# A first depthwise convolution on TensorE: two taps a matmul from stacked copies of the padded image

## The reference

```
xin = jnp.einsum('bchw,oc->bohw', x, in_proj_w)
xc = jax.nn.silu(_dwconv(xin, conv2d_w, conv2d_b))
x1 = _dwconv(xc, dw_w, dw_b)
```

## Time and profile before

| what | value |
|---|---|
| three executions | 2455.08, 2449.93, 2454.44 us |
| median | 2454.44 us |
| the profiled execution | 2455.15 us |
| its span, first to last instruction | 2453.3 us |
| mean granted TensorE clock | 0.941 of full speed |
| TensorE busy | 2144.5 us (87%) |
| VectorE busy | 1864.1 us (76%) |
| first depthwise convolution, first pair | about 484 to 592 us |

### The profile page before, as it was taken

One profiled execution on the slowest core, in us unless ns is written; L12 is line 12 of the kernel. 1 busy time (PEld: TensorE's weight loads), 2 busy tenths in 40 slices (PEclk: granted clock), 3 DMA queues, 4 the chain that ended last, 5 costly groups with the idle time before them and its releaser, 6 DMA issues. The chain is left out here.

```text
span 2453.3 us, 28912 instructions
## 1 busy us (share of the span) xinstructions
PE 2144.5 (87%) x7243; PEld 1122.6 (46%) x7243; DVE 1864.1 (76%) x3251; ACT 1434.4 (58%) x2268; POOL 1412.1 (58%) x1287
## 2 busy tenths in 40 slices
PE   2998869898998999997988987698979799999798
PEld 2397635443453444433335964353435334444243
DVE  6556767589986999995755668565999589999754
ACT  1843444286884777773346446335868567777632
POOL 2232008488977999982322400393989399999532
PEclk9989989999998999998997998799999899999899
DMA  5000192500001222225810005634000012212344
GB/s 188 1 1 1 48 339 82 176 39 0 1 1 23 43 44 57 44 52 161 232 41 0 1 0 195 215 106 166 1 1 1 11 22 44 61 39 56 91 119 114
DMA packets 199338, 172.76 MB, mean 70 GB/s; under 512 B 72535, under 2 KB 175327, under 8 KB 195831
## 3 DMA queue, kind: packets, MB, share of 16 engines
q1 hardware_dynamic: 199159, 170.78, 24.3%
HBM read 81.69 MB, written 72.29 MB: 63 GB/s over the span
## 5 line engine op out<-in xcount | busy, mean ns | idle before, releaser
L942 POOL TENSOR_TENSOR BIG<-BIG 128x512 f32<-128x512 f32 x320 | 407.1, 1272 | 91.9 <-DVE BIG L850 73.5
L850 DVE TENSOR_TENSOR BIG<-PSUM,BIG 128x512 f32<-128x512 f32 x576 | 390.8, 681 | 61.0 <-PE PSUM L1061 35.5
L1133 DVE SCALAR_TENSOR_TENSOR PSUM<-BIG,VECS,PSUM 128x1024 f32<-128x1024 f32 x224 | 288.2, 1286 | 37.0 <-PE PSUM L2112 31.8
L776 POOL TENSOR_TENSOR BIG<-TOEP,BIG 128x384 f32<-128x384 f32 x84 | 98.0, 1194 | 320.2 <-DVEq L1558 320.2
L1069 PE MATMUL PSUM<-BIG,CSTS 128*128 128x512 f32 x512 | 264.9, 598 | 0.0
L2112 PE MATMUL PSUM<-BIG,WDW 128*128 128x512 f32 x512 | 233.0, 599 | 13.8 <-ACT BIG L2012 13.8
L1061 PE MATMUL PSUM<-BIG,SELB 120*128 120x512 bf16 x576 | 210.6, 384 | 16.9 <-issue 10.1
L2291 PE MATMUL PSUM<-BIG 128*128 128x381 f32 (+1 forms) x576 | 189.4, 492 | 12.9 <-DVE BIG L783 12.9
L1061 PEld LDWEIGHTS PSUM<-BIG,SELB 120*128 120x128 bf16 x576 | 55.1, 96 | 262.0 <-DVE BIG L850 163.3
L2112 PEld LDWEIGHTS PSUM<-BIG,WDW 128*128 128x128 f32 x512 | 97.1, 192 | 141.0 <-issue 115.0
L1785 POOL TENSOR_TENSOR BIG<-BIG 128x1024 f32<-128x1024 f32 x64 | 151.0, 2360 | 10.3 <-POOL BIG L1788 10.3
(11 more groups left out here) (365 smaller groups left out, 5170.9 us busy)
## 6 DMA issues: line engine op xcount, KB each, us to landing
spill<-X SPq DMA_DIRECT2D x18, 1024.0 KB, 5.9
back_spill<-BIG SPq DMA_DIRECT2D x32, 576.0 KB, 3.4
X<-x SPq DMA_DIRECT2D x32, 512.0 KB, 7.9
rows_spill<-X SPq DMA_DIRECT2D x64, 256.0 KB, 4.0
out<-BIG SPq DMA_DIRECT2D x64, 256.0 KB, 3.6
BIG<-rows_spill SPq DMA_DIRECT2D x28, 512.0 KB, 5.2
X<-back_spill SPq DMA_DIRECT2D x14, 896.0 KB, 11.7
BIG<-fc SPq DMA_DIRECT2D x8, 1024.0 KB, 10.3
```

Source lines behind the costliest of these rows:

```text
L776: eng.tensor_tensor(to.rearrange("p (x c r) -> p x c r", x=3, r=WROW), TOEP[:, y].unsqueeze(1).unsqueeze(1).broadcast_to([P, 3, WCH, WROW] ...
L850: dve.tensor_tensor(img(product_buffer(b, q)), img(PSUM[:, (k + q) % 2, :]), pch(c, XBASE, dy, dx), ALU.mult).then_inc(df_p, 1)
L942: pool.tensor_tensor(a, a, x, ALU.add).then_inc(df_add, 1)
L1133: return dve.scalar_tensor_tensor(out=rows8(to), in0=strip(c, base, dy, dx), scalar=vc(weights, j), in1=rows8(acc), op0=ALU.mult, op1=ALU.add)
```

## The change

Taps 0 and 1 of every strip now go to TensorE together with taps 3 and 4. For each strip, four DMAs on SP's queue copy PAD rows into a buffer `STK[c % 2]`, each 64 partitions by 8 rows of 130 elements: for image q, partitions 0 to 63 get the rows shifted up by one and partitions 64 to 127 get the rows themselves. A matmul over 128 partitions with the weights `WSTK` (128 x 64: the diagonal of tap j above, that of tap j + 3 below) then sums two taps of one image into 64 partitions of PSUM. The two images go to the two halves of TensorE's columns, in turn. TensorE waits for the DMAs (`moved`) in place of `in_cp`. The DMAs of strip c wait for `in_cp` of that strip and for `d1_mm` of strip c - 2. Four of the nine reloads of X are issued at once as before, the other five stand one each behind the copies of strips 0 to 4.

ScalarE keeps two side taps, 2 and 5, GpSimd one addition. VectorE has taps 6, 7, 8 and the side sum in every strip, and waits for `in_cp` of the strip below itself. The buffers are placed anew in REG, and the counts of the semaphores change with them.

```diff
-SIDE_TAPS = 3
-DW1_VECTOR, DW2_VECTOR = (4, 5), (5, 6)
+DW1_STACK, DW1_SIDE, DW1_LAST = (0, 1), (2, 5), (6, 7, 8)
+SIDE_TAPS = len(DW1_SIDE)
+DW1_VECTOR, DW2_VECTOR = (len(DW1_LAST) + 1,) * 2, (5, 6)
...
+BACK_FIRST = 4
...
-MOVES = [n + PARTS3 * 32 for n in SPREAD]
+STACKED = NS // 2 * 64
+MOVES = [n + STACKED + PARTS3 * 32 for n in SPREAD]
...
-        DW1_FIRST = [SIDE_TAPS + n - 1 for n in DW1_VECTOR]
-        WDW1 = sb("WDW1", [P, NTAP - min(DW1_FIRST), P])
+        WSTK = sb("WSTK", [P, len(DW1_STACK), C])
...
-        d_xb, d_sq, d_tap = (r.take(STRIP) for _ in range(3))
+        d_xb, d_sq = (r.take(STRIP) for _ in range(2))
+        tap_at = 2 * (2 * 8 * PW + SIDE_TAPS * STRIP)
+        assert r.at <= tap_at
+        r.at = tap_at
+        d_tap = r.take(STRIP)
         d_side = r.take(2, STRIP)
-        r.at = l2at
+        r.at = 0
+        STK0 = r.take(2, 8 * PW)
         a_side = r.take(SIDE_TAPS, 2, STRIP)
+        STK = (STK0, r.take(2, 8 * PW))
...
+        def stacked(pair, c):
+
+            return pair * MOVES[c % 2] + SPREAD[c % 2] + (c // 2 + 1) * 64
...
-                for w in range(WINDOWS):
+                def back(w):
+
                     lo, hi = (0 if w == 0 else 1), (WROW if w == WINDOWS - 1 else WROW - 1)
                     sp.dma_start(X[:, STEP * w + lo:STEP * w + hi, :].rearrange("p r x -> p (r x)"),
                                  back_spill[w, :, lo * W:hi * W]).then_inc(l1_back if w == 0 else x_in[(w - 1) // 2], 16)
+
+                for w in range(BACK_FIRST):
+                    back(w)
+                for c in range(NS):
+                    sp.wait_ge(in_cp, strip_done(pair, c))
+                    settle(sp)
+                    if c >= 2:
+                        sp.wait_ge(d1_mm, strip_done(pair, c - 2))
+                        settle(sp)
+                    for q in range(2):
+                        for up in range(2):
+                            first = BASE + c * 8 + up - 1
+                            sp.dma_start(STK[c % 2][up * C:(up + 1) * C, q, :].rearrange("p (r w) -> p r w", w=PW),
+                                         PAD[q * C:(q + 1) * C, first:first + 8, :]).then_inc(moved[c % 2], 16)
+                    if c + BACK_FIRST < WINDOWS:
+                        back(c + BACK_FIRST)
...
-            for w, name, first in ((WDW1, "conv2d_w", min(DW1_FIRST)), (WDW2, "dw_w", min(DW2_FIRST))):
-                for j in range(first, NTAP):
-                    dve.tensor_scalar(w[:, j - first, :], ident, vc(name, j), None, ALU.mult)
+            for j in range(min(DW2_FIRST), NTAP):
+                dve.tensor_scalar(WDW2[:, j - min(DW2_FIRST), :], ident, vc("dw_w", j), None, ALU.mult)
+            for n, j in enumerate(DW1_STACK):
+                for up in range(2):
+                    rows = slice(up * C, (up + 1) * C)
+                    dve.tensor_scalar(WSTK[rows, n, :], ident[rows, rows], vc("conv2d_w", j + 3 * up)[rows], None, ALU.mult)
...
                 for c in range(NS):
                     n = DW1_VECTOR[c % 2]
+                    dve.wait_ge(in_cp, strip_done(pair, min(c + 1, NS - 1)))
                     dve.wait_ge(d1_mm, strip_done(pair, c))
...
-                            add_tap(dve, c, SIDE_TAPS + j, BASE, "conv2d_w", d1_acc(c), d1_acc(c)).then_inc(d1_tap, 1)
+                            add_tap(dve, c, DW1_LAST[j], BASE, "conv2d_w", d1_acc(c), d1_acc(c)).then_inc(d1_tap, 1)
...
-                    pool.wait_ge(d1_side, d1_side_done(pair, c, 2))
-                    pool.wait_ge(d1_part, d1_part_done(pair, c, 0))
-                    pool.tensor_tensor(a_side[:, 0, c % 2, :], a_side[:, 0, c % 2, :], a_side[:, 2, c % 2, :],
-                                       ALU.add).then_inc(d1_part, 1)
...
-                    for j in range(SIDE_TAPS):
+                    for n, j in enumerate(DW1_SIDE):
                         dy, dx = TAPS[j]
-                        act.activation(rows8(a_side[:, j, c % 2, :]), strip(c, BASE, dy, dx), ACT.Identity,
+                        act.activation(rows8(a_side[:, n, c % 2, :]), strip(c, BASE, dy, dx), ACT.Identity,
                                        scale=vc("conv2d_w", j)).then_inc(d1_side, 1)
...
-                    pe.wait_ge(in_cp, strip_done(pair, min(c + 1, NS - 1)))
+                    pe.wait_ge(moved[c % 2], stacked(pair, c))
                     if c >= 3:
                         pe.wait_ge(d1_act, strip_done(pair, c - 3))
-                    conv(d1_acc(c), WDW1, min(DW1_FIRST), c, BASE, DW1_FIRST[c % 2]).then_inc(d1_mm, 1)
+                    for h in range(2):
+                        for n, j in enumerate(DW1_STACK):
+                            dx = TAPS[j][1]
+                            for q in range(2):
+                                rows = STK[c % 2][:, q, :].rearrange("p (r w) -> p r w", w=PW)
+                                ins = pe.matmul(img(d1_acc(c)[q * C:(q + 1) * C, h * CH:(h + 1) * CH]), WSTK[:, n, :],
+                                                rows[:, h * ROWS:(h + 1) * ROWS, 1 + dx:1 + dx + W], start=(n == 0),
+                                                stop=(n == len(DW1_STACK) - 1))
+                    ins.then_inc(d1_mm, 1)
```

More of the change, by code:

```diff
@@ L437, in parts_moved @@
         def parts_moved(pair, n):
-            return pair * MOVES[n % 2] + SPREAD[n % 2] + (n // 2 + 1) * 64
+            return pair * MOVES[n % 2] + SPREAD[n % 2] + STACKED + (n // 2 + 1) * 64
+        def stacked(pair, c):
+            return pair * MOVES[c % 2] + SPREAD[c % 2] + (c // 2 + 1) * 64
         def strip_done(pair, c):
@@ L1143, in side_order @@
             for c in range(NS):
-                yield from ((1, c, 0), (1, c, 1))
+                yield (1, c, 0)
                 for strips, (s, j) in zip(sum(SIDE_AHEAD, ()), ahead):
@@ L1151, in program, with d1_part_done @@
         part_at = {step: n for n, step in enumerate(side_order())}
-        assert len(part_at) == NS * (2 + SIDE_STEPS)
-        def d1_part_done(pair, c, j):
-            return pair * (NS * (2 + SIDE_STEPS)) + (part_at[1, c, j] + 1)
+        assert len(part_at) == NS * (1 + SIDE_STEPS)
+        def d1_part_done(pair, c):
+            return pair * (NS * (1 + SIDE_STEPS)) + (part_at[1, c, 0] + 1)
         def d2_side_done(pair, c, j):
-            return pair * (NS * (2 + SIDE_STEPS)) + (part_at[2, c, j] + 1)
+            return pair * (NS * (1 + SIDE_STEPS)) + (part_at[2, c, j] + 1)
         @block.vector
@@ L1590, in _ @@
                         if j < n - 1:
-                            add_tap(dve, c, SIDE_TAPS + j, BASE, "conv2d_w", d1_acc(c), d1_acc(c)).then_inc(d1_tap, 1)
+                            add_tap(dve, c, DW1_LAST[j], BASE, "conv2d_w", d1_acc(c), d1_acc(c)).then_inc(d1_tap, 1)
                         else:
-                            dve.wait_ge(d1_part, d1_part_done(pair, c, 1))
+                            dve.wait_ge(d1_part, d1_part_done(pair, c))
                             dve.tensor_tensor(d1_acc(c), d1_acc(c), a_side[:, 0, c % 2, :], ALU.add).then_inc(d1_tap, 1)
```

## The result

The changed kernel takes 2468.52 us (median of four, 2465.68 to 2470.64) against 2452.28 us for the kernel before in the same series: ratio 1.0055, 95% interval 1.0041 to 1.0069. It is 16 us slower. I had forecast 8 us faster, with a range that ended at 2466. The profiled execution has a span of 2468.6 us, 15.3 more than before.

What follows compares the result with a forecast made beforehand. TensorE was taken as the bound at 6.00 us a strip, VectorE just behind. Winning 4.2 us a pair, 8.4 for two, brought the profiled 2455.15 to 2446.8 and the median to 2446 us; range 2426 to 2466.

Steps and rivals of the forecast that it cites:

- The halves of TensorE's columns overlap: TensorE's stacked matmuls: 16 records a strip on alternating column halves run together, 3.44 us; no overlap had chance 0.07.
- The pace afterwards: TensorE, strips 6 to 15 of the first depthwise convolution: 1.72 + 3.44 + 0.2 = 5.36 us a strip.
- The copies' rate: SP's queue: a strip's four copies, 1.065 MB, take 4.8 us at 222 GB/s; forecast case given chance 0.38.
- The wait of two buffers: Copies wait for TensorE two strips back: a 6.5 us round gives 5.05 us a strip, hidden under 5.36.
- While they last, the queue needs 4.8 + 2.2 = 7.0 us a strip: SP's queue at the stage's start: copies plus one reload at 425 GB/s, so TensorE waits in strips 1 to 5.
- The sum: First pair: TensorE starts at 491.1, VectorE's last strip ends at 588.5 against 591.9; 4.2 us taken as won a pair.
- Range and sign: Whole kernel: 2426 to 2466 us; chances faster 0.61, same 0.16, slower 0.23.
- a low rate of the copies as such: Rival on SP's queue: four copies take over 5.1 us, nothing won at 5.36, 2462 us at 5.6; chance 0.30.

Runs made afterwards that it cites:

- the other order of the copies: Changed kernel with a strip's four copies issued lower to lower, upper to upper, lower to upper, upper to lower half of the partitions: 2468.98 us, ratio 1.0068.
- short reloads: Changed kernel with the five reloads of X among the copies moving one row of each window in place of 14 or 15: 2440.53 us, ratio 0.9945.
- all reloads first: Changed kernel with all nine reloads of X issued ahead of the copies (BACK_FIRST 9 in place of 4): 2468.2 us, ratio 1.0051.
- reloads and copies apart: Changed kernel with SP waiting for each landing in strips 0 to 4, so a reload and copies never share the queue: 2509.02 us.
- kept warm: Changed kernel with three spare 128x512 matmuls on TensorE before the wait for copies in strips 1 to 5: 2474.62 us, ratio 1.007.
- the halves apart: Changed kernel with TensorE summing all of image 0 of a strip, then image 1, in place of alternating matmuls: 2509.14 us.

## Why the prediction was wrong

- **The halves of TensorE's columns overlap**: right. 16 records take 3.65 us with the last one's tail (3.6 forecast).
- **The pace afterwards**: 5.50 us against 5.36. The changes between all and half of the columns cost 0.34 a strip in place of the 0.2 I took. From 539.00 to 542.58 is 3.58 for 3.44 of work, and from 537.08 to 539.00 is 1.92 for 1.72. Over ten strips that is 1.4 us a pair.
- **The copies' rate**: right, and the number on which I said the forecast hung. 229 GB/s and 4.65 us, against 222 and 4.8. The Trainium skill's SBUF — State Buffer, "Door 1: The DMA port swizzle", has 196 GB/s for a transfer of 1 MiB on 64 partitions and about 218 as the limit without its fixed time; these copies are a sixth above the first and 5% above the second. The same page of the Trainium skill, "Can I just issue two DMAs to hit both halves?", has two DMAs on the two halves at only 6% over one. That the other order of the copies brought nothing that can be told from the spread agrees with it, as far as that run goes.
- **The wait of two buffers**: right, it hides at this pace (short reloads, all reloads first), but with little to spare: four copies take 7.0 us from their issue to the start of the strip, not 6.5, and the last two strips, which have no projection between them, wait 1.5 and 1.8 us.
- **"While they last, the queue needs 4.8 + 2.2 = 7.0 us a strip"**: this is the step that failed. I added the reload's time alone (2.2 us at 425 GB/s) to the copies' time alone. Measured are 8.8 us a strip, 44.0 for strips 1 to 5 where I had 35: 9.0 us in the first pair, and 43.3 and 8.3 in the second. Two parts are seen. The plain sum is 7.3 (reloads and copies apart), 0.3 more than I had. The other 1.5 a strip come with the sharing, in which the engines are as busy as ever and move 236 GB/s on average. The mean of the two transfers at their own rates would be 1.98 MB / 7.3 us = 271. The single DMA packets in the traces (of 7168 or 7680 bytes for the reloads, 4160 for the copies) say which of the two slows down. With only reloads in the queue (all reloads first, 482 to 494 us) a reload's packet takes 274 ns on average, 2.2 us of all 16 engines for a reload. Among the copies (the changed kernel, 490 to 530 us) it takes 458 ns, 3.7 us a reload. A packet of the copies takes 298 ns there and 290 without reloads, 4.8 and 4.6 us a strip. So the term that was wrong is the reload's 2.2; 4.8 + 3.7 = 8.5 is nearly all of the 8.8. Spread over every second strip the reloads' packets still took 414 ns (490 to 530 us), so a reload cost nearly as much there. The halved clock has no share that can be seen in the first pair, and at most 1.7 us in the second (kept warm).
- **The sum**: VectorE ends at 597.6, 9.1 after the 588.5 of the forecast. Strip 0 starts 1.6 us before the 491.1 of the forecast; strips 1 to 5 cost 9.0 more; strips 6 to 15 take 55.1 in place of 53.6, 1.5 more; the last strip's end 0.2 more. That strip 0 was early is chance: this execution came to the stage 2.2 us sooner, and counted from the issue of the reloads strip 0 is 0.6 late.
- **Range and sign**: I had given slower 0.23, but for a low rate of the copies as such. No rival had the interplay of the two kinds of transfer. No row before showed a mix, and I put a single value on it; the matrices' 230 GB/s for both together, 8.6 us a strip, could have been tried as a bound. That 2466 was missed by only 2.5 us says nothing for the range: its upper end stood for copies at a lower rate, which did not come.

Shown by the runs: the reloads' traffic among the copies costs 28 us (short reloads), some 15 of them by the sharing (an estimate: 1.5 us in ten strips); the round of waits costs nothing, the clock little, and the order of the copies nothing that could be told. Why a reload's packets slow down among copies is not shown. The Trainium skill's SBUF — State Buffer, "Door 1: The DMA port swizzle", has a transfer on 64 partitions on 8 of the 16 ports; that the copies hold ports which a reload needs too would fit, but it was not separated from a cost of changing between transfers on each engine.

## What to carry to other kernels

Times of two kinds of transfer, each measured alone, fell short here of what both took in one queue, 7.3 us against 8.8. Counting the fast one at the slow one's rate while both are in the queue would have given 4.65 + 4.0 = 8.65 us. So take that as the bound, and have the fast one pass first only if something else can fill the time: by itself that won nothing here. A new transfer that is hidden in the steady state can still cost more than it wins at the start of a stage, where the queue is full of what the stage before left. Where the start is full, do the first pieces in the old way, without the new resource: it turned 16 us lost into 10 won.

## What was not expected of the hardware

With the halves apart, a strip's matmuls took 5.42 us, 11 steps of 0.43 to 0.48 and a last record of 0.59, where 16 steps were expected. The single records show why: four start alone, from 541.38 us on; at 543.15 two start within 5 ns; from then on they come in pairs, four pairs in all, and the last four are alone again. The records don't name their image; the reading that fits is that TensorE began with image 1 beside image 0's fifth record, although the sixth to eighth stood ahead of it in the program. In this run the halves overlapped only over these four records, so they should be alternated; but they overlap without being neighbours.
